# A fused cross-attention and expert kernel on one Trainium2 core: the down product of 28 of 32 token groups made transposed, 448 columns at a time

## The reference

```
x1  = x + softmax((LN(x) Wq + bq)(ctx Wk + bk)^T / 16) (ctx Wv + bv)     x: 16 x 112 x 256, ctx: 16 x 375 x 256
y   = LN(x1)                                                             1792 tokens of 256
cw  = softmax(y w_router) * softmax(y w_gating / 0.1), divided by its sum over the 8 experts
out = x1 + sum over e of cw[:, e] * (silu(y w_gate[e]) * (y w_up[e])) w_down[e]      8 experts, 1024 hidden features
```

## Time and profile before

| | |
|---|---|
| runs | 980.57 to 981.32 us, median 981.25 us |
| the profiled execution | 981.21 us, its span 979.4 us |
| PE busy | 971.5 us (99%), granted clock 0.999 |
| DVE, POOL, ACT busy | 745.7 us (76%), 671.1 us (69%), 482.9 us (49%) |
| attention and plain quads | about the first 150 us |
| the quads 4 to 63 | about 150 us to 963 us |

### The profile page before, as it was taken

How to read it: one execution, slowest core, us unless ns; L and a number is a source line. 1 busy time by engine, 2 the same in 40 slices (tenths; PEclk the granted TensorE clock), 3 DMA queues, 4 the chain that set the end, 5 groups by cost and what they waited for, 6 DMA issues and landing times.

```text
span 979.4 us, 16565 instructions
## 1 busy us (share of the span) xinstructions
PE 971.5 (99%) x6193; PEld 927.3 (95%) x6193; DVE 745.7 (76%) x1353; ACT 482.9 (49%) x853; POOL 671.1 (69%) x514
## 2 busy tenths in 40 slices
PE   8999999999999999999999999999999999999998
PEld 7999999999999999999999999999999999999998
DVE  6987446877778777788777887777877778777785
ACT  6897554454444444544535444444445454444441
POOL 4799876776757676667667675766766676757642
PEclk9999999999999999999999999999999999999999
DMA  9250140010001010010101010010101010100002
GB/s 227 81 152 20 49 143 23 22 44 16 29 22 44 23 36 30 22 45 22 44 2 43 23 44 22 22 44 23 44 22 32 13 45 22 44 22 23 1 1 76
DMA packets 37352, 40.63 MB, mean 41 GB/s; under 512 B 2644, under 2 KB 35272, under 8 KB 37272
## 3 DMA queue, kind: packets, MB, share of 16 engines
q1 hardware_dynamic: 37264, 39.58, 13.6%
q10 hardware_dynamic: 8, 0.00, 0.0%
HBM read 35.90 MB, written 3.67 MB: 40 GB/s over the span
## 4 chain that ended last, share of the span: by engine, by line
PE 97%; DMA 2%; ACT 0%; SPq 0%; POOL 0%; issue 0%; DVE 0%; DVEq 0%
PE ps L272 94%; DMA shared<-in_ctx 1%; PE ps L1527 1%; PE ps L1615 1%; DMA xf<-in_L_xattn_Wk 1%; PE ps L1555 0%; PE ps L1602 0%; PE ps L1572 0%; PE ps L1516 0%; POOL arena L413 0%; SPq L286 0%; DVE xsacc L1236 0%; ACT arena L647 0%; ACT arena L701 0%; PE ps L1473 0%
## 5 line engine op out<-in xcount | busy, mean ns | idle before, releaser
L272 PE MATMUL ps<-arena 128*128 128x256 f32 (+4 forms) x3120 | 413.7, 284 | 0.2
L272 PEld LDWEIGHTS ps<-arena 128*128 128x128 f32 (+2 forms) x3120 | 403.2, 189 | 6.3 <-POOL arena L480 0.2
L480 POOL TENSOR_TENSOR arena<-shared,arena 128x448 fp32r<-128x448 f32 x196 | 251.0, 1294 | 191.4 <-ACT arena L808 185.6
L272 PE MATMUL ps<-xc_hi,w_hi 128*128 128x448 f32 x904 | 331.9, 367 | 0.0
L272 PE MATMUL ps<-xc_hi,w_lo 128*128 128x448 f32 x904 | 330.2, 365 | 0.0
L272 PE MATMUL ps<-xc_lo,w_hi 128*128 128x448 f32 x904 | 329.7, 365 | 0.0
L801 ACT ACTIVATE shared<-shared 128x448 f32<-128x448 f32 x180 | 101.4, 579 | 192.0 <-DVE shared L1176 125.0
L272 PEld LDWEIGHTS ps<-xc_hi,w_lo 128*128 128x128 f32 x904 | 169.8, 188 | 13.8
L272 PEld LDWEIGHTS ps<-xc_hi,w_hi 128*128 128x128 f32 x904 | 170.6, 189 | 10.2
L272 PEld LDWEIGHTS ps<-xc_lo,w_hi 128*128 128x128 f32 x904 | 170.6, 189 | 10.1
L1170 DVE TENSOR_TENSOR shared<-ps,shared 128x448 f32<-128x448 f32 x60 | 37.5, 625 | 110.8 <-PE ps L272 110.8
(11 more groups left out here) (145 smaller groups left out, 1098.7 us busy)
## 6 DMA issues: line engine op xcount, KB each, us to landing
early<-in_L_ffn_w_down SPq DMA_DIRECT2D x16, 512.0 KB, 4.0
shared<-in_ctx SPq DMA_DIRECT2D x16, 336.0 KB
w_raw<-in_L_ffn_w_gate SPq DMA_DIRECT2D x17, 256.0 KB, 2.9
w_raw<-in_L_ffn_w_up SPq DMA_DIRECT2D x17, 256.0 KB, 3.2
early<-in_L_ffn_w_gate SPq DMA_DIRECT2D x15, 256.0 KB, 2.8
early<-in_L_ffn_w_up SPq DMA_DIRECT2D x15, 256.0 KB, 3.1
x_dram<-xsacc SPq DMA_DIRECT2D x8, 224.0 KB, 3.7
xsacc<-x_dram SPq DMA_DIRECT2D x1, 1792.0 KB, 7.6
```

The source lines that it names most:

```text
L272: ins = nc.tensor.matmul(dst, w, m, start=first and i == 0, stop=last and i == len(passes) - 1, skip_group_check=onto)
L480: nc.gpsimd.tensor_tensor(h[:, 1, j, at:at + TC], tile, h[:, 0, j, at:at + TC].bitcast(fp32), ALU.subtract).then_inc(hid_lo_done, 1)
```

## The change

The groups 2 to 29 (`TURNED`) get their down product transposed. `unit(g, k)` makes 128 output features for 448 tokens: w_down is the stationary operand (128x128), hidden the moving one (448 columns), 12 matmuls. Four units make a group. `weigh` on DVE multiplies a unit out of PSUM with a row of combine weights that lies in all partitions (`cw_all`), into one of two buffers `weighed`; `add_unit` on POOL adds that to `acc_t` in SBUF. For the first group of each half `weigh` writes `acc_t` directly.

```diff
+            def unit(g, k):
+                u = UNITS * (g - CP) + k
+                c, block = 1 - k // 2, slice(k % 2 * P, (k % 2 + 1) * P)
+                if k == 0:
+                    pe.wait_ge(wd_done, g // CP + 1)
+                    pe.wait_ge(hid_lo_done, 4 * (FPAIRS * (g + 1) - 1) + HID21)
+                if k == 2:
+                    pe.wait_ge(hid_lo_done, 4 * FPAIRS * (g + 1))
...
+                        passes += three(wd[:, 0, t, block], wd[:, 1, t, block], h[:, 0, j, toks], h[:, 1, j, toks])
+                accumulate(ps_unit[u % 2], passes).then_inc(unit_ready, 1)
+            def weigh(g, k):
+                u = UNITS * (g - CP) + k
+                c = 1 - k // 2
+                ve.wait_ge(unit_ready, u + 1)
...
+                    at_least(ve, unit_done, u - 2 - UNITS * CP + 1)
+                    to = weighed[u % 2]
+                nc.vector.tensor_tensor(to, ps_unit[u % 2], cw_all[:, g % CP, c * TC:(c + 1) * TC], ALU.mult).then_inc(weighed_done, 1)
+            def add_unit(g, k):
+                if g < 2 * CP:
+                    return
...
+                to = unit_at(g, k)
+                nc.gpsimd.tensor_tensor(to, to, weighed[u % 2], ALU.add).then_inc(unit_done, 1)
```

The order of PE in a quad becomes this for the turned groups (the parts for the last two quads are cut):

```diff
                 gate_1_6_5(n)
-                if n % FPAIRS:
+                if odd and by_tile:
                     down(g, 2)
-                else:
+                if not odd and g - 1 not in TURNED:
                     down(g - 1, 5)
                 up_1_6_5(n)
+                if odd and turned:
+                    unit(g, 2)
                 gate_2_7(n)
                 up_2_7(n)
+                if odd and turned:
+                    unit(g, 3)
                 gate_4_3(n)
-                if n % FPAIRS:
+                if odd and by_tile and n < QUADS - 1:
                     down(g, 4)
+                if not odd and turned:
+                    unit(g, 0)
                 up_4_3(n)
+                if not odd and turned:
+                    unit(g, 1)
```

```diff
+                if n == QUADS - 2:
+                    turn_back(0, 0)
...
+                if cp == 0 and i < 2:
+                    pe.wait_ge(weighed_done, UNITS * len(TURNED) - 1 + i)
...
+            down(g, 4)
+            down(g, 5)
+            pe.wait_ge(act_done, last + HID11)
+            turn_back(1, 2)
+            down(g, 6)
+            turn_back(1, 3)
```

More of the change, by code:

```diff
@@ L35, in xattn_ffn_kernel @@
     HSLOTS = 4
+    TURNED = range(CP, GROUPS - CP)
+    UNITS = 4
+    BY_TILE = {g: i for i, g in enumerate([g for g in range(GROUPS) if g not in TURNED])}
     SCALE = float(D) ** -0.5
@@ L106, in xattn_ffn_kernel @@
         ones = xf_f[:, 3 * DK * D:3 * DK * D + TQ]
+        cw_all = xf_f[:, 0:CP * TH].rearrange("p (c t) -> p c t", c=CP)
+        weighed = [xf[:, 4 + i, :] for i in range(2)]
         xc_hi = sb("xc_hi", [P, CP, 7, TC], fp32r)
@@ L122, in xattn_ffn_kernel @@
         w_raw1 = early[:, FT * D:].rearrange("p (m s f) -> p m s f", m=2, s=8)
+        last_acc = [v[:, 0:RT * D].rearrange("p (i d) -> p i d", i=RT) for v in
+                    (early[:, FT * D:], w_raw0[:, :, :, :].rearrange("p m s f -> p (m s f)"))]
         at0 = 0
@@ L602, in quad @@
                     low_set(2 * hn + 2)
+                if n % FPAIRS and g in TURNED:
+                    add_unit(g, 2)
                 low_hidden(n, HID11, g11, 0, 0)
@@ L974, in quad @@
                 hn, turn = n // (CP * FPAIRS), n % (CP * FPAIRS)
+                if turn == 2 and hn > 1:
+                    high_down(hn)
                 gate_first(n)
@@ L1430, in _ @@
             sums_1_3(1)
+            keep_cw()
             def quad(n):
@@ L1435, in quad @@
                 gate_u2(n)
-                if odd:
+                if odd and g in TURNED:
+                    weigh(g, 0)
+                    weigh(g, 1)
+                elif odd:
                     add_rows(g, 0, ps_r[0])
                     add_rows(g, 1, ps_r[1])
+                elif g - 1 in TURNED:
+                    weigh(g - 1, 3)
                 else:
@@ L1441, in quad @@
                     add_rows(g - 1, 5, ps_r[5])
+                if n == QUADS - 2:
+                    add_back(0, 0)
                 up_u2(n)
+                if n == QUADS - 2:
+                    add_back(0, 1)
                 gate_u3_c22(n)
-                if odd:
+                if odd and g in TURNED:
+                    weigh(g, 2)
+                elif odd:
                     add_rows(g, 2, ps_r[2])
                     add_rows(g, 3, ps_r[3])
+                if n == QUADS - 2:
+                    add_back(0, 2)
+                if n == QUADS - 1:
+                    add_back(1, 0)
                 up_u3_c22(n)
-                if not odd:
+                if not odd and g - 1 not in TURNED:
                     add_rows(g - 1, 6, ps_r[6])
+                if n == QUADS - 2:
+                    add_back(0, 3)
                 gate_c21_c12(n)
@@ L1461, in _ @@
                 quad(n)
-            for i in range(4, RT):
-                add_rows(GROUPS - 2, i, ps_r[i])
+            add_back(1, 1)
+            add_rows(GROUPS - 2, 4, ps_r[4])
+            add_rows(GROUPS - 2, 5, ps_r[5])
+            add_back(1, 2)
+            ve.wait_ge(back_ready[1], 4)
+            add_rows(GROUPS - 2, 6, ps_r[6])
+            add_back(1, 3)
             for i, made in ((4, 2), (5, 2), (0, 4), (1, 4), (2, 6), (3, 6), (6, RT)):
@@ L1603, in transpose_norm2, with route, transpose_logits @@
                 ins.then_inc(x2t_ready, 1)
[L1605 to L1617 removed]
+            def route(cp, c):
+                pe.wait_ge(wr_done, 1)
+                pe.wait_ge(part_lo[cp, "first" if c == 0 else "second"], 1)
+                if (cp, c) == (1, 1):
+                    pe.wait_ge(second7_lo, 1)
+                if cp == 0:
+                    pe.wait_ge(pt_lo_done, 2 * (PAIRS - 1) + c + 1)
+                else:
+                    pe.wait_ge(lt_kept, c + 1)
+                accumulate(ps_lt[c], [(wr_split[:, k - 1, :, :].rearrange("p l n -> p (l n)"), x[:, cp, PLAIN_A[c + 1, k], :])
+                                      for k in (1, 2) for x in (xc_hi, xc_lo)]).then_inc(lt_ready, 1)
+            def transpose_logits(cp):
+                pe.wait_ge(lt_kept, 2 * (cp + 1))
+                if cp == 0:
+                    pe.wait_ge(mix_done, PAIRS)
+                else:
+                    pe.wait_ge(logits_done, cp)
+                for i in range(RT):
+                    ins = nc.tensor.transpose(ps_l[:, i, :, :].rearrange("p l n -> p (l n)"), lt_f[:, i * P:(i + 1) * P], ident[0:4 * E, 0:4 * E])
+                ins.then_inc(logits_ready, 1)
             def keep_busy(n):
```

657 lines of the change are left out of this document (389 added, 268 removed).

## The result

The changed kernel takes **1004.75 us** (median of four runs, 1002.24 to 1006.94) against 981.08 for the kernel before beside it: ratio 1.0242, interval 1.0228 to 1.0257. Slower, as forecast, but three times as much: 988.8 was predicted, 7.6 us more, and 1004.75 lies above the range too.

The account below looks back on a forecast made before the run. PE was taken as the bound, busy 971.5 of 979.4 us. Terms -8.7 + 13.5 + 3.0 + 1.2 + 1.1 - 0.2 + 0.8 - 1.1 - 2.0 = +7.6 on 981.2 gave 988.8 us; eight-in-ten range 974.5 to 995.

Parts of the forecast that it names:

- rival C: Quads with low_down at the head: low_hidden 21 comes late, 0.5 us in 14 quads, 996 us in all; chance 0.12.
- The units, -8.7: Down products: four units of 448-column matmuls replace seven down rows, saving 0.31 us in each of 28 groups.
- The wait, +13.5: Even quads 8 to 60: PE's product 7 of gate waits 0.50 us for gate_u2, 27 times.
- Quad 4, +0.8: Start of quad 4: PE waits for keep_cw, the combine weights' copy on DVE, where no wait was before.
- The attention and the router, -3.1: Before the quads: router with 448-column matmuls and transposes -1.1 us, new attention order -2.0 us.
- One wait of 1 us and part of the fillers: Attention's start: what the new order was to remove, taken as -2.0 us, bounds -5 and +3.
- The ends, +5.1: Ends of the quads: transposes +3.0, quad 62's turn_back wait +1.2, last add_back wait +1.1, POOL's last wait -0.2 us.
- Rival A: Even quads: DVE's hidden12 comes before POOL's low_hidden, so the gate_u2 wait does not come; 974.7 us, chance 0.20.

Follow-up runs that it names:

- experiment 5: Changed kernel with unit 3 behind gate_4_3, combine weights turned early, and GpSimd's low_down waiting until VectorE has ended hidden12: 979.74 us, ratio 0.9994.
- experiment 3: Changed kernel with turn_cw ahead of plain(3, 0, 3) on PE and keep_cw ahead of plain_hidden(3, 3) on VectorE: 1000.51 us, ratio 1.0196.
- experiment 1: Changed kernel with unit 3 of odd quads moved behind gate_4_3 in PE's order: 1005.3 us, ratio 1.0255.
- experiment 4: Changed kernel with both edits, unit 3 behind gate_4_3 and the combine weights turned early: 1003.26 us, ratio 1.0228.
- experiment 6: experiment 5 with add_back(1, 1) on VectorE right behind hidden22 of quad 63, ahead of its hidden12: 977.49 us, ratio 0.9971.
- Experiments 8 to 11: On experiment 6: router weights loaded after x 977.78 us, that without two fillers 976.55, old load order 980.74; on the kernel before: router weights loaded earlier 981.4.
- experiment 2: Kernel before, with down rows 4, 5 and 6 ahead of gate_4_3 of the odd quad, no units or GpSimd adds: 1002.3 us, ratio 1.0228.
- experiment 7: experiment 2 with GpSimd's low_hidden 11 of odd quads waiting until VectorE has done hidden12: 1005.9 us, ratio 1.0259.

## Why the prediction was wrong

**Right.** PE sets the time, the wait for `gate_u2` replaces the slack of 3.36 us, in 27 even quads, where it starts 4.1 behind their start; `hidden12` of 1.57 is its reason; POOL's and ACT's new work costs nothing (rival C did not come); and the sign. The Trainium skill (TensorE: Matmul & The Clock Gate, Back-to-back issue gap) gives its formula for the gap of a single matmul, and by it the groups would gain 0.09 each. The runs differ: 0.34 in experiment 5, and the runs decide.

**The units, -8.7.** They give 9.5 (27.09 - 26.75 in experiment 5). Within the 0.5 that was allowed, nearly.

**The wait, +13.5, is the term that failed most.** Its place, count and cause were right, its price was not. It was taken as the late start of one product, 0.50. Measured, that start is 0.52 late and the next one 0.10 more, and two quads are 27.36 with the wait and 26.75 without: 0.61 each, 16.5 in all; the upper bound in the text, 0.65, was nearer. And a term was missing altogether: behind ten of the 27 waits PE goes on 2% slower until the next, 27.78 - 27.36 = 0.42 each, +4.2. In the 27 pairs from quad 8 on that makes -27 x 0.34 + 16.5 + 4.2 = +11.5, and +11.6 stands in the account. The forecast for the same two terms was -8.7 + 13.5 = +4.8.

**Quad 4, +0.8.** PE waited 2.3 us. "DVE's last step before it" was given 0.53 us to the start of the next, as in the kernel before; here that is 1.47 (149.35 to 150.82), since the step takes 1.55 next to a POOL operation. That is the very effect from which the main wait was worked out, not applied here. PE also went on 0.50 behind the copy, where 0.06 had been taken. The low clock behind it, +1.5, was not in the sum: 3.8 in all where 0.8 was forecast. In experiment 3 the wait is gone and the median 4.2 lower, with runs that lie several us apart.

**The attention and the router, -3.1.** The idle of 4.8 did not go. In the profiled execution 0.3 of it went and 0.7 of work; in the five executions of experiments 1 and 3 to 6, with the same front, the idle was 0.9 to 3.2 above that of before. "One wait of 1 us and part of the fillers" had no row behind it. In experiments 3 to 6 quad 4 begins 2.2 to 3.6 us later than before, so that the new front costs where -3.1 was forecast. The -1.0 of the account was the lucky end. Experiments 8 to 11 show that the router's load doesn't do it and that the old order of loads is worse; the cause stays open. Open too is where the median's distance to the profiled execution comes from, 2.5 us. The start is one candidate, the number of slow stretches another. It is not the clock alone: the four executions had 0.998, 0.997, 0.998 and 0.995 of it on average, and the third, with as much as the first, took 3.7 us longer.

**The ends, +5.1.** 6.5 measured. Of the waits, that of quad 62 has 1.0 of idle (1.2 forecast) and the last 1.8 (1.1 forecast). With 3.0 for the transposes that leaves 0.7; 0.3 of it is in quad 6, where two starts of PE lie 0.40 and 0.31 behind the one before, at 190.3 us, in every version of the new scheme.

**Taken together** the profiled execution is 13.5 us above the 7.6 of the forecast: 6.8 in the quads (wait and pace), 3.0 at quad 4, 2.1 in attention and router, 1.4 at the ends, 0.2 without a place.

**Rival A** was given 0.20 and did not come, but its mechanism is real: experiment 5 makes VectorE come first and lands at 979.74, with the rival's 974.7 missed by the start (quad 4 begins 3.0 us later than before, and not 2.3 earlier) and the last wait. What I did not see is that the order of the two engines could be chosen.

**Open.** Why PE keeps the 0.2067 pace after some waits and not after others. Experiment 3 shows it after six of its 27 waits of the same size, experiment 4 after two of 13, experiments 1 and 2 after none. In the quads 8 to 61 every such stretch begins within five matmuls of a wait for `gate_u2` and ends at the next wait. But a wait isn't needed: in experiment 5, which has none there, eleven distances behind the transposes of quad 62 are 0.2067 on average too (940.40 to 942.68 us). No run was made for it alone.

## What to carry to other kernels

When matmuls are reordered, list for each semaphore on PE the work that used to stand ahead of it: down rows put elsewhere, with no work added (experiment 2), cost 2.3%, about as much as the whole change (2.4%). Price a new wait of PE by the starts of matmuls across a wait that the trace has, not by the idle beside it, and keep PE free of waits of 2 us: behind four of nine here the clock was at half for some 3 us. Where a VectorE operation on two SBUF tiles sets the path, look at what GpSimd has in front of it; if GpSimd has slack right there, make it wait. Make sure that it has: in experiment 7 it had none, and PE then waited for GpSimd.

## What the runs showed that was not expected

- One and the same VectorE operation (`hidden12`, 128x448) takes 0.61, 1.57 or 2.83 us, as it comes first, behind a GpSimd operation of 1.2 us, or behind one of 2.8. A little more or less time can turn the order round: experiment 1 made PE's wait four times as long by giving VectorE more time.
- After a wait of 0.35 us, matmuls of 448 columns start 0.2067 us apart in place of 0.2027 for the next 27 us, at a granted clock of 1.00, in ten cases of 27 in the changed kernel and six of 27 in experiment 3.
- Of nine waits of PE of 1.8 to 2.2 us behind 145 us (changed kernel, experiments 1, 3, 4 and 5), four were followed by some 3 us at a granted clock near 0.5, and five were not.
- A wait of 0.35 us by its row costs 0.61 by the starts.
